# A six-layer decoder on one core: the last two sequences of test-time training drain in an order of their own, and the cross-attention's first keys and values load earlier

## What is computed

```python
# test-time training, per sequence, 32 heads of 8; ys is the output of the scan over chunks
Z1_bar = xq @ W1_s - eta_mb * Attn1 @ grad + b1_bar
out = xq + _ln(Z1_bar, ln_w, ln_b)            # norm per head
...
out = _ln(out, post_norm_weight, post_norm_bias)   # over the 256 features
return out @ o_w.T
...
x = _layernorm(x + _L0_attn_ref(...), axis=-1)
# cross-attention, 32 query heads, 8 key heads of 8 features
scores = jnp.einsum('bkgsd,bktd->bkgst', qh, kh) / scale
weights = jax.nn.softmax(scores, axis=-1)
out = jnp.einsum('bkgst,bktd->bkgsd', weights, vh)
x = _layernorm(x + _L0_xattn_ref(x, ctx_512, ctx_512), axis=-1)
```

## Time and profile before

| | us |
|---|---|
| median of 3 runs | 1366.75 (1365.1 to 1367.13) |
| the profiled execution, its own time | 1371.59 |
| its span, first to last instruction | 1369.8 |
| TensorE busy | 1209.4 (88%) |
| DVE busy | 961.5 (70%) |
| ACT busy | 549.9 (40%) |
| POOL busy | 251.7 (18%) |
| mean granted clock of TensorE | 0.95 of full |

### The profile page before, as it was taken

One profiled execution on the slowest core, in us unless ns is written; L12 is line 12 of the kernel. 1 busy time (PEld: TensorE's weight loads), 2 busy tenths in 40 slices (PEclk: granted clock), 3 DMA queues, 4 the chain that ended last, 5 costly groups with the idle time before them and its releaser, 6 DMA issues. The chain is left out here.

```text
span 1369.8 us, 24619 instructions
## 1 busy us (share of the span) xinstructions
PE 1209.4 (88%) x9163; PEld 783.6 (57%) x9163; DVE 961.5 (70%) x2191; ACT 549.9 (40%) x1473; POOL 251.7 (18%) x327
## 2 busy tenths in 40 slices
PE   8799999999968888888988989987999999789965
PEld 3577788677733333345555457775777777334432
DVE  1699988699956777668984999873447688753325
ACT  3111112444415666664542210013777777233212
POOL 4000000122210111304331000110000000137851
PEclk9899999999969999999999989997999999899987
DMA  6111213100011232070001000006600000449556
GB/s 190 48 47 51 74 55 107 13 2 2 2 58 58 70 109 81 24 142 1 1 1 62 2 1 1 2 1 197 187 17 17 24 21 20 122 147 285 103 112 254
DMA packets 82850, 92.88 MB, mean 68 GB/s; under 512 B 25232, under 2 KB 66214, under 8 KB 82470
## 3 DMA queue, kind: packets, MB, share of 16 engines
q1 hardware_dynamic: 73820, 77.16, 18.8%
q0 software_dynamic: 6784, 10.43, 4.2%
q10 hardware_dynamic: 2128, 3.71, 0.8%
HBM read 68.91 MB, written 22.36 MB: 67 GB/s over the span
## 5 line engine op out<-in xcount | busy, mean ns | idle before, releaser
L390 DVE TENSOR_REDUCE gqa_x_slots<-gqa_scores 128x8 f32<-128x1024 f32 x64 | 78.3, 1226 | 40.6 <-PE gqa_scores L277 40.5
L1488 DVE TENSOR_REDUCE mla_neg_max<-mla_scores 128x8 f32<-128x1024 f32 x32 | 39.2, 1225 | 88.3 <-PE mla_scores L1359 62.6
L1437 ACT ACTIVATE mla_probs<-mla_scores,mla_neg_max 128x128 f32<-128x128 f32 x256 | 90.0, 385 | 6.2 <-DVE mla_neg_max L1488 6.1
L298 PE MATMUL gqa_scoresT<-gqa_x_slotsT,gqa_keys 32*128 32x512 f32 x256 | 72.0, 634 | 19.7 <-issue 14.7
L2160 PE MATMUL ttt_z_ps<-ttt_prod,ident 128*128 128x256 f32 x288 | 73.9, 416 | 8.9 <-DVE ttt_prod L2236 8.9
L347 ACT ACTIVATE gqa_expT<-gqa_scoresT 128x1024 f32<-128x1024 f32 x64 | 65.5, 1024 | 39.7 <-PE gqa_scoresT L298 39.7
L277 PE MATMUL gqa_scores<-gqa_keys_bd,xT 32*128 32x512 f32 x256 | 70.7, 640 | 1.4 <-DVE gqa_x_slots L390 1.4
L2160 PEld LDWEIGHTS ttt_z_ps<-ttt_prod,ident 128*128 128x128 f32 x288 | 57.6, 207 | 22.9 <-DVE ttt_prod L2236 14.6
L1349 PE MATMUL mla_q_ps<-xT,mla_to_keys 128*128 128x128 f32 x512 | 65.7, 284 | 1.5 <-PEq L63 1.5
L1349 PEld LDWEIGHTS mla_q_ps<-xT,mla_to_keys 128*128 128x128 f32 x512 | 62.7, 200 | 2.2 <-issue 2.1
L2167 PE MATMUL ttt_w_ps<-ttt_prod,ttt_neg_ident 128*128 128x144 f32 x448 | 58.8, 291 | 4.9 <-DVE ttt_prod L2269 4.9
(11 more groups left out here) (441 smaller groups left out, 2845.7 us busy)
## 6 DMA issues: line engine op xcount, KB each, us to landing
...
```

The costliest lines, as they stand in the source:

```text
L298: ins = nc.tensor.matmul(scoresT[:, j % 2, :], keys[group, b % NBUF, c, :], x_slotsT[group, k % 2, :], start=True, stop=True)
L390: nc.vector.tensor_reduce(x_slots[:, b % 2, :, c * NJ + 2 * half:c * NJ + 2 * half + 2, HD].rearrange("p g j -> p j g"), scores[:, of].rea ...
L1437: ins = nc.scalar.activation(probs[:, k % NB, e, i, :], scores[:, k % 2, e, i, :], ACT.Exp, bias=neg_max[:, k % 2, e, i:i + 1], accum_out= ...
```

## The change

Five edits go together.

1. The buffers of the cross-attention for sequence 0 are made first in the program, by the new class `CrossFirst`, and SP loads them in the output part. In the cross-attention SP begins with sequence 1, TensorE has no wait for the keys of sequence 0, and its four fillers are gone.
2. DVE clears the two buffers of `x_slots` one after the other; POOL fills the first as soon as that one is clear. DVE still waits for both.
3. DVE has an order of its own in steps 16 and 17: variance(15) directly behind block_norm(13), and post_norm ahead of vector_end.
4. ACT takes the root of sequence 15 ahead of norm.scalar(13) and copy_res(14) in step 17, and copies res(15) ahead of norm.scalar(14) in step 18.
5. TensorE transposes `res` ahead of norm.tensor from step 16 on. The transposes of sequences 14 and 15 and the product of sequence 15 go to a free bank, `z_ps[:, 0]`, and out(15) has no wait for the statistics of sequence 14. Three pairs of fillers (128x512) are added: ahead of turn_res(14), behind out(14) and behind out(15).

```diff
+class CrossFirst:
+    def __init__(self, nc, ctx, io):
+        ...
+        self.loads = [(self.keys_bd[:], io["gqa_keys_bd"][0]), (self.keys[:], io["gqa_keys"][0]), (self.values[:], io["gqa_values"][0])]
...
         @block.sync
         def _(sp):
-            for b in range(B):
+            for b in range(1, B):
...
         @block.gpsimd
         def _(pool):
-            pool.wait_ge(slots_clear, 1)
-
             def fill(b):
+                pool.wait_ge(slots_clear, min(b + 1, 2))
...
                 if c == 0 and half == HIGH:
-                    pe.wait_ge(loaded[b % NBUF], 48 * (b // NBUF + 1))
+                    need(pe, loaded[b % NBUF], 48 * (b // NBUF + (b % NBUF > 0)))
...
-            keep_busy(nc, weighted_ps[:], keep["ident"][:], keep["xT"][:, 0, 0:512], 4)
...
-            nc.vector.memset(x_slots[:], 0.0).then_inc(slots_clear, 1)
-            dve.wait_ge(slots_clear, 1)
+            for i in range(2):
+                nc.vector.memset(x_slots[:, i], 0.0).then_inc(slots_clear, 1)
+            dve.wait_ge(slots_clear, 2)
...
+            out_of = lambda b: z_ps[:, 0, 0:D] if b == B - 1 else out_ps
+            res_of = lambda b: z_ps[:, 0, D:2 * D].rearrange("p (c t) -> p c t", c=DH) if b >= B - 2 else resT_ps
+
+            @block.sync
+            def _(sp):
+                for dst, src in cross.loads:
+                    sp.dma_start(dst, src).then_inc(cross_loaded, 16)
+                sp.wait_ge(cross_loaded, 16 * len(cross.loads))
...
                     if live(b):
                         add_beta(b, par)
+                    if b == B + 1:
+                        deviation(b - 2)
+                    if b == B + 2:
+                        copy_res(b - 3)
                     if live(b - 4):
                         norm.scalar(act, b - 4)
-                    if live(b - 3):
+                    if live(b - 3) and b != B + 2:
                         copy_res(b - 3)
-                    if live(b - 2):
+                    if live(b - 2) and b != B + 1:
                         deviation(b - 2)
...
                 def out(b):
                     need(pe, resT_copied, b + 1)
-                    need(pe, norm.var_ready, b)
+                    if b < B - 1:
+                        need(pe, norm.var_ready, b)
...
+                def go_on(count):
+                    keep_busy(nc, scores[:, 0].rearrange("p n j i -> p (n j i)"), keep["ident"][:], k_feat[:, 0, 0:512], count)
...
                         unit(apply, b, par, u, APPLY_LAG)
+                        if u == 2 and b == B:
+                            go_on(2)
+                        if u == 2 and live(b - 2) and b >= B:
+                            turn_res(b - 2)
                         if u == 2 and live(b - 3):
                             norm.tensor(pe, b - 3)
-                        if u == 2 and live(b - 2):
+                        if u == 2 and live(b - 2) and b < B:
                             turn_res(b - 2)
                         if u == 3 and live(b - 2):
                             out(b - 2)
+                            if b >= B:
+                                go_on(2)
...
                 def step(b, par):
+                    if b == B:
+                        post_stats(b - 2)
+                        block_norm(b - 3)
+                        variance(b - 1)
+                        post_norm(b - 2)
+                        norm.vector_end(dve, b - 3)
+                        head_norm(b - 1)
+                        residual(b - 1)
+                        return
+                    if b == B + 1:
+                        post_stats(b - 2)
+                        block_norm(b - 3)
+                        post_norm(b - 2)
+                        norm.vector_end(dve, b - 3)
+                        return
```

41 lines of the change are left out of this document (23 added, 18 removed).

## The result

| | before | after |
|---|---|---|
| median of the timed runs | 1370.51 us (20 runs, 1365.1 to 1379.18) | 1362.63 us (20 runs, 1355.45 to 1372.09) |
| the profiled execution | 1371.59 | 1355.45 |
| its span | 1369.8 | 1353.6 |
| its mean granted clock | 0.950 | 0.963 |

The ratio is 0.9948, with a 95% interval of 0.9932 to 0.9964: 7.1 us less, between 4.9 and 9.3. The forecast was 8.35 us less and a time of 1358.4. Against the twenty runs beside it the change of the time came out close to that; the time itself is 4.2 us higher than forecast, and 3.8 of these are the base: the three runs shown before had a median of 1366.75, the twenty beside the changed kernel 1370.51. Against the 1366.75 that the forecast started from, the changed kernel is only 4.1 us lower, half of what was forecast.

The account below looks back on a forecast made before the run. Bound: 26 us from the output part's dense work to the first cross-attention scores, two sequences' tails in single file, TensorE mostly at half clock. Drain -4.7, entry -5.55 and +1.9 give -8.35: 1366.75 to 1358.4 us; range 1355.5 to 1363.2.

Parts of the forecast that it names:

- (e): Entry to the cross-attention: the clock falls around 399 and returns about 406 to 407, costing +1.9 us.
- (c): Drain of the output part: at full clock, TensorE's transposes and product are shorter, -1.45 us.
- (a): Drain: root of sequence 15 ahead of ACT's two copies, so DVE's reciprocal starts earlier, -2.06 us.
- (b): Drain: post-normalisation of sequence 15 ahead of sequence 14's normalisation no longer waits for POOL or that operation, -1.19 us.
- (d): Entry to the cross-attention: four fillers and the wait for first keys go, DVE's two clearings are on the path, -5.55 us.
- A: The forecast itself: full clock in the drain, half clock for 5 to 10 us at the entry; 1357.5 to 1359.5, chance 0.60.
- C: Rival: the clock falls in the drain in spite of the fillers, drain ends at about 402; 1362.3 us, chance 0.12.
- B: Rival: at the entry the clock does not fall, or only for a moment; -10.2, 1356.5 us, chance 0.13.
- D: Rival: drain at full clock, cross-attention start too thin for the clock's return before 416 to 420; 1361 us, chance 0.07.
- F: Rival, slower: fillers at half clock hold the drain at its old end and the entry runs cold; 1369.5 us, chance 0.02.
- E: Rival: another wait holds DVE in the drain where the root did; -5, 1362 us, chance 0.04.

Follow-up runs that it names:

- e5: The changed kernel with ACT's root of sequence 15 put back behind the two copies; one run, 1379.53 us.
- e6: The changed kernel with DVE's normalisation of sequence 14 put back ahead of the post-normalisation of sequence 15; one run, 1374.25 us.
- e3: The changed kernel without its three pairs of fillers in the drain; ratio to the kernel before 0.9952.
- e2: The changed kernel's new cross-attention entry only, with the drain of the kernel before; ratio to the kernel before 0.9948.
- e1: The changed kernel's drain only, with the cross-attention entry of the kernel before; ratio to the kernel before 0.9946.
- e7: The changed kernel plus a fourth key/value buffer, two fillers behind the first scores, and POOL clearing half of x_slots; ratio to the kernel before 0.988.

## Why the prediction was right, and where it was not

The terms of the drain and of the clearing came out; two steps failed. The larger miss is the base, to which the difference was applied: 3.8 us. The other is term (e), the cost of the clock at the entry: 1.9 us forecast, 3.1 measured. And the full clock in the drain, on which (c) rests, is not secure: it held in five of nine profiles with the fillers.

**The root of sequence 15 (a).** -2.06 forecast, 6.07 - 3.85 = 2.22 measured. The variance stood right behind block_norm(13) and the root had come back when DVE wanted it. e5 undid it alone and got the wait back, longer than before.

**The order of the norms (b).** -1.19 forecast. The post-normalisation came 3.42 earlier behind the mark, less 2.22: 1.20. The product of sequence 14 was there in time, as forecast. e6 undid it alone: 1.2 later.

**Full clock in the drain (c).** -1.45 forecast; ACT's end came 4.97 earlier, less 3.42: 1.55. By e3 it needs the fillers: ACT's end is 2.4 us later without them, more than (c), since at half clock the post-normalisation too comes 0.9 later. The fillers cost 1.88 to 1.98 a pair, not 1.7, and at full clock still stood in nobody's way: the second pair ended at 388.48, and the transposes started at 388.85, once post_norm(15) was through. The price had been halved from 6.71 us of eight records, the last of which already ran at full clock.

**The entry (d).** -5.55 forecast, 10.59 - 4.97 = 5.62 measured. The two clearings are the bound, as forecast; e2 shows the same 3.75 us with the old drain. But two parts of the term were off and cancelled. The first clearing starts 1.74 us behind ACT's end, not 1.94, and the first maximum comes 2.01 behind that start, not 1.86. The term took its price from the length of the row, 0.86 ns an element, and the rows of 0.91 for 1024 elements look alike; but the second clearing starts 1.07 us behind the first, in all nine profiles that have two (1.07 or 1.08), which is 1.05 ns an element. So the length of the row is less than what a clearing costs. (The single row of 2048 starts 1.94 behind ACT's end and the first of 1024 1.74, which would put the missing time ahead of the row; that is an inference.) The Trainium skill (VectorE: DVE Perf Modes, "Zero memsets can be issued as uint32 (trn2)") has one cycle per element, by the prediction's estimate 2.1 us for 2048; the starts agree with it (2 times 1.07), and the length of the row does not. What made the sum come out is that in before the single clearing ended 3.70 us behind ACT's end (404.01 + 1.76 - 402.07), and the two together end 3.72 behind it (397.50 + 0.91 - 394.69).

**The clock at the entry (e): the term that was mis-sized.** +1.9 forecast, +3.1 measured. That the clock would fall was right. It stayed low from 397.0 to 407.3, by the means of 0.76 in 396 to 398 and 0.68 in 406 to 408: about 10 us rather than 7. (That the entry would be cold was also the rule of the Trainium skill, TensorE: Matmul & The Clock Gate, "What's actually happening", which has throttled as the default; the trace agrees, 0.50 from 398 to 406.) The step that failed is "the high half of the second scores is hidden behind DVE's two maxima". It took half a score as half of the 1.14 us of eight records. Alone, the four records of a half take 1.13 at full clock already, and 2.07 at half. The profile of before has this row, which I had not read:

```profile
412.73 1.13 PE L277 MATMUL gqa_scores<-gqa_keys_bd,xT 32*128 32x512 f32 x4 [1.40 <-DVE gqa_x_slots L390]
```

At half clock this half is not covered by the maximum of 1.23 us, and the transposes of the slots (1.11) and the next half come behind it: DVE waits 1.05 and 1.83. With 3.1 the sum is -4.97 - 5.62 + 3.1 = -7.5, as the tenth maximum shows. The timed 7.1 us agree with that within their interval.

**The base: the step that failed first.** "The difference carries over as it is: 1366.75 - 8.35" took a median of three runs for the kernel's time, and most of the miss in the time itself is there. I took the 2.0 us by which three runs differed for the scatter of medians. Twenty runs of the kernel before lie between 1365.1 and 1379.18, and their median is 3.8 us above that of the three. Beside the experiments, on three chips, the same kernel has medians of 1367.49, 1370.6 and 1372.83 us. The range allowed 1 us for this. The difference of 16.1 us between the two profiled executions is not the change's either: 2.4 of it lie ahead of the mark; 10.4 lie from the mark to the last maximum of the cross-attention (566.3 against 553.5, less 2.4), of which 2.9 come behind the tenth maximum, where the waits for loads fell from 3.6 to 0.6; the other 3.3 lie behind, where the change does nothing.

**The rivals.** A is what the profiles of after show, both times. C, the clock falling in the drain in spite of the fillers, got 0.12, and happened in four of nine profiles with fillers. The forecast did not name what goes with it, a low clock far ahead, from 200 to 290 us; that one causes the other is not shown. Its price was too high: I had all three pairs at half clock and the drain's end back at its old place, 4.6 us later than forecast; only the first pair was slow, and the end came 2.4 us later (e1, e7; in e5 and e6, where the clock fell twice, the third pair took 2.4 and 3.1 too).

How often it happens in the timed runs no profile says, but their granted clocks give a hint: the four profiles in which it fell have a mean of 0.942 to 0.947, the five in which it held 0.957 to 0.963, and of the twenty runs of after five have 0.943 to 0.949 and 1367.6 us or more, the others 0.953 or more and at most 1365.24. At a quarter, the mean gain at the tenth maximum would be, as an estimate, 7.5 - 0.25 x 2.4 = 6.9 us, at a half 6.3, counting the drain alone and without what the loads may give; the interval holds both.

B did not occur in any profile. D and F did not in after: the clock came back 11 us behind the entry's first scores. But the start of the cross-attention can be too thin for the clock, as D had it, in other kernels: in e3 it came back 18.7 us behind the first scores and in e5 19.9, within D's 17 to 21, and the first ten maxima took 21.9 and 22.5 us, 5.3 and 5.9 over 16.6. In e3 the clock was low from the drain on; in e5 it was full again from 405.9 to 412.7 and fell 2.9 us behind the first scores. E is refuted by the reciprocal, which waits for nothing.

**What stays open.** Why the halves of the change timed as low as the whole. Whether the steadier loads are part of the change's gain: waits of 0 to 2.1 us in the kernels with three buffers and the new entry against 3.6 in one profile of before, and 1.6 in e1, which has the old one. And why the clock dips between 200 and 290 us in some executions.
